# First sublayer's delta rule: one product per doubling step, two per chain step with the state turned, filter products in the last half of the chain

## The reference

```
A = where(strict_low, -einsum('bhnid,bhnjd->bhnij', kb, k), 0)
T = solve_triangular(eye - A, eye, lower=True, unit_diagonal=True)
u = T @ v
w = T @ kb
def step(S, inp):
    attn = where(low, q @ k.T, 0)
    u_i = u - w @ S
    o_i = q @ S + attn @ u_i
    S = S + k.T @ u_i
fir_s = dwconv_causal(v, fir_short_filt)   # 5 taps
fir_l = dwconv_causal(v, fir_long_filt)    # 64 taps
```

## Time and profile before

| what | value |
|---|---|
| median of 3 runs | 3429.51 us (3428.8 to 3432.13) |
| the profiled execution's own time | 3426.57 us |
| its span in the profile | 3424.8 us |
| the stage, from its first matmul to its last copy | 112.7 to 354.5 us |
| granted TensorE clock, mean of the span | 0.878 of full speed |
| PE busy, share of the span | 81% |
| DVE / ACT busy, share of the span | 53% / 40% |

### The profile page before, as it was taken

How to read it: one execution, slowest core, us unless ns; L and a number is a source line. 1 busy time by engine, 2 the same in 40 slices (tenths; PEclk the granted TensorE clock), 3 DMA queues, 4 the chain that set the end, 5 groups by cost and what they waited for, 6 DMA issues and landing times. The chain is left out here.

```text
span 3424.8 us, 57880 instructions
## 1 busy us (share of the span) xinstructions
PE 2778.6 (81%) x22862; PEld 1420.1 (41%) x22862; DVE 1825.0 (53%) x3512; ACT 1380.9 (40%) x2682; POOL 765.7 (22%) x721
## 2 busy tenths in 40 slices
PE   6665778778888768889858889899888988777986
PEld 3454336623336633334332222243233443654546
DVE  4311135369885368830178887611396454537733
ACT  3310434353224337662347777633303233234552
POOL 1000004426535420000245440000361000240003
PEclk8766778978888979999979999999799998887987
DMA  2023001212101231000040220000160001022102
GB/s 114 15 58 85 1 0 43 55 45 74 62 19 46 84 74 33 23 2 0 0 74 15 32 32 1 1 0 12 40 157 13 1 1 50 14 59 69 35 9 74
DMA packets 84405, 130.25 MB, mean 38 GB/s; under 512 B 15584, under 2 KB 52928, under 8 KB 82856
## 3 DMA queue, kind: packets, MB, share of 16 engines
q1 hardware_dynamic: 71528, 106.68, 11.4%
q0 software_dynamic: 9152, 16.71, 2.0%
q10 hardware_dynamic: 3456, 3.15, 0.3%
HBM read 99.93 MB, written 25.85 MB: 37 GB/s over the span
## 5 line engine op out<-in xcount | busy, mean ns | idle before, releaser
L1787 DVE TENSOR_REDUCE at_mp<-PS 128x1 f32<-128x384 f32 (+3 forms) x640 | 306.7, 536 | 85.0 <-PE PS L1610 72.6
L1736 ACT ACTIVATE at_pt<-PS 128x384 f32<-128x384 f32 (+3 forms) x704 | 270.3, 455 | 190.2 <-PE PS L1610 156.5
L1602 PE MATMUL PS<-at_kx,at_qx 48*128 48x384 bf16 (+5 forms) x640 | 198.6, 347 | 60.6 <-DVE at_mp L1787 21.6
L1630 PE MATMUL PS<-at_qx,at_kx 57*128 57x512 bf16 (+5 forms) x704 | 192.8, 314 | 9.7 <-ACT at_pt L1736 9.4
L4235 ACT ACTIVATE ls_pt<-PS,ls_far 128x512 f32<-128x512 f32 x256 | 155.5, 685 | 24.8 <-PE PS L4056 17.9
L4382 DVE CUSTOM_DVE_ANT_0 PS<-PS,ls_pt 128x1024 f32<-128x1024 f32 x128 | 153.9, 1239 | 19.4 <-ACT ls_pt L4235 16.5
L1610 PE MATMUL PS<-at_above,identb 64*128 64x128 bf16 (+1 forms) x1408 | 160.7, 212 | 0.0
L1610 PE MATMUL PS<-at_other,at_eye 64*128 64x128 bf16 (+1 forms) x1408 | 158.2, 208 | 0.0
L2507 DVE TENSOR_TENSOR_SCAN mb_ring<-PS,mb_ring 128x1024 f32<-128x1024 f32 x64 | 146.6, 2291 | 19.3 <-POOL mb_ring L2446 6.7
L2462 PE MATMUL PS<-mb_ring,ident 128*128 128x512 f32 x256 | 149.1, 736 | 5.9 <-DVE mb_ring L2512 5.9
L1113 DVE SCALAR_TENSOR_TENSOR X<-PS,small_L,X 128x512 f32<-128x512 f32 x8 | 6.0, 751 | 261.2 <-PE PS L1061 261.2
(11 more groups left out here) (833 smaller groups left out, 6527.2 us busy)
## 6 DMA issues: line engine op xcount, KB each, us to landing
rw_arena<-rw_v_rows SPq DMA_DIRECT2D x32, 512.0 KB, 4.6
dl_arena<-in_fir_bank SPq DMA_DIRECT2D x32, 256.0 KB, 3.1
lnA<-mb_rows SPq DMA_DIRECT2D x16, 512.0 KB, 3.6
XN<-mb_rows SPq DMA_DIRECT2D x16, 512.0 KB, 3.4
ffn_place<-in_ffn_L SPq DMA_DIRECT2D x4, 1152.0 KB, 17.1
x_rows<-mx_t SPq DMA_DIRECT2D x16, 256.0 KB, 2.4
mx_s<-y_rows SPq DMA_DIRECT2D x16, 256.0 KB, 4.7
ffn_place<-in_ffn_L SPq DMA_DIRECT2D x4, 1024.0 KB, 9.2
```

The source lines that it names most:

```text
L1602: mm = nc.tensor.matmul(PS[:, n % 3, 0:e - c], QX[rows, u % 3, g, blk(i, P)], KX[rows, u % 3, g, c:e], start=True, stop=True)
L1630: mm = nc.tensor.matmul(PS[:, 3 + n % 3, 0:e - c], KX[rows, u % 3, g, blk(j, P)], QX[rows, u % 3, g, c:e], start=True, stop=True)
L1736: nc.scalar.activation(PT[:, y % SLOTS, g, 0:e - c], PS[:, 3 + n % 3, 0:e - c], ACT.Exp, scale=SCALE).then_inc(exp_done, 1)
L1787: nc.vector.tensor_reduce(best, sc, AX.X, ALU.max).then_inc(s_maxed, 1)
```

## The change

`build` makes one product for each step. The square of A is no longer made on PE: ACT copies the square of A' out of the double, and DVE turns it with a 32x32 transpose (`fix`, s = 1 to 4), which gives A squared. Steps 2, 3 and 4 are now one double each. M and G take the places of kb and q side by side (`KBQ`), the outputs go to another buffer (`OD`).

In the chain, PSUM holds the state turned and the output beside it, 64 columns: `corrections(n)` makes u against k and the attention matrix in one set of 8 matmuls, `chain(n)` adds S against M and G in another 8. DVE turns the first half into S (`carry`, a transpose where a copy was) and copies the outputs of each chunk. `corrections(n+1)` is issued right behind `chain(n)`.

The sixteen filter products are taken out of the second half and put behind the links 16 to 31 (`LATER = 16`), on two PSUM banks in turn instead of one. The text of SP's program is not changed, but what it waits for comes later.

```
@@ -2957,10 +2957,10 @@
-        M, U = KBC, VC
+        OD, U = KBC, VC
-        G, OD, S = Q, KB, KK
+        M, G, S = KB, Q, KK
...
@@ -3176,10 +3176,11 @@
-        PRODUCTS = (1, 1, 2, 2, 2, 1, 1, 1)
-        ON_DVE = (4, 1, 2, 2, 1, 1, 0, 2)
+        ON_DVE = (4, 1, 2, 2, 2, 1, 0, 2)
         ON_ACT = (0, 1, 1, 1, 1, 0, 2, 0)
+        ONE_EACH = (1,) * STEPS
+        LATER = 16
...
+            firs_at = lambda n: (n - LATER,) if 0 <= n - LATER < 2 * STEPS else ()
+
+            def carried(n):
+                return PS[:, 4 + n % 2, 0:4 * CH].rearrange("p (b a i) -> p b a i", b=2, a=2)
...
@@ -3260,11 +3252,10 @@
+                    elif s == 1:
+                        single(lo, pw[:, 0, :], pt[:, 0, 0, :])
                     elif s <= 4:
-                        single(hi, pt[:, n % 2, 0, :], pw[:, n % 2, :])
-                        if s in (2, 3):
-                            double(lo, pw[:, n % 2, :], pt[:, n % 2, :, :])
-                        elif s == 4:
-                            single(lo, pw[:, n % 2, :], pt[:, n % 2, 1, :])
+                        double(lo, pw[:, old, :], pt[:, old, :, :])
...
-                def chain(n):
+                def corrections(n):
                     if n % CHUNKS == 0:
                         pe.wait_ge(fixed, upto(ON_DVE, 2 + n // CHUNKS, STEPS - 1))
+                        pe.wait_ge(copied, upto(ON_ACT, 2 + n // CHUNKS, STEPS - 1))
+                    if n >= 2:
+                        pe.wait_ge(o_taken, n - 1)
                     for b in range(2):
                         for h in rows:
+                            mm = nc.tensor.matmul(carried(n)[h, b, :, :], U[h, chunk(b, n)], KA[h, :, chunk(b, n)], start=(b == 0), stop=(n == 0), skip_group_check=True)
+                    return mm
+
+                def chain(n):
+                    pe.wait_ge(s_done, n)
+                    for b in range(2):
+                        for h in rows:
+                            mm = nc.tensor.matmul(carried(n)[h, b, :, :], S[h, chunk(b, n)], KBQ[h, :, chunk(b, n)], start=False, stop=True, skip_group_check=True)
                     mm.then_inc(ks_ready, 1)
+                    if n + 1 < NSTATE:
+                        corrections(n + 1)
...
                 def fir(i):
                     if i == 0:
                         pe.wait_ge(window_done, STEPS)
-                    else:
-                        pe.wait_ge(fir_done, i)
+                    if i >= 2:
+                        pe.wait_ge(fir_done, i - 1)
...
                 for s in range(STEPS):
-                    build(1, s)
-                    chain(2 * s)
-                    fir(2 * s)
-                    build(3, s)
-                    chain(2 * s + 1)
-                    fir(2 * s + 1)
-                for n in range(CHUNKS, NSTATE - 1):
+                    for half, u in enumerate((1, 3)):
+                        n = 2 * s + half
+                        build(u, s)
+                        if n:
+                            chain(n)
+                        else:
+                            first()
+                        for i in firs_at(n):
+                            fir(i)
+                for n in range(CHUNKS, NSTATE):
                     chain(n)
+                    for i in firs_at(n):
+                        fir(i)
...
@@ -3383,62 +3376,50 @@
+                    elif s <= 4:
+                        dve.wait_ge(copied, upto(ON_ACT, u, s))
+                        nc.vector.transpose(pw[:, s % 2, :], pt[:, s % 2, 0, :]).then_inc(fixed, 1)
                         nc.vector.tensor_tensor(c3(pt[:, s % 2, 1, :]), c3(pt[:, 1 - s % 2, 1, :]), half(1), ALU.add).then_inc(fixed, 1)
...
                 def carry(n):
                     dve.wait_ge(ks_ready, n + 1)
+                    if n + 1 < NSTATE:
+                        s = S.rearrange("p (b t) -> p b t", b=2)[:, :, blk(n + 1, CH)]
+                        nc.vector.transpose(s, carried(n)[:, :, 0, :]).then_inc(s_done, 1)
+                    nc.vector.tensor_copy(OD.rearrange("p (b t) -> p b t", b=2)[:, :, blk(n, CH)], carried(n)[:, :, 1, :]).then_inc(o_taken, 1)
```

More of the change, by code:

```diff
@@ L3311, in chain, with first @@
                     mm.then_inc(ks_ready, 1)
-                    if n > CHUNKS:
-                        outputs(n - 1)
+                    if n + 1 < NSTATE:
+                        corrections(n + 1)
+                def first():
+                    corrections(0).then_inc(ks_ready, 1)
+                    corrections(1)
                 def fir(i):
@@ L3322, in fir @@
                         for c in range(PIECE):
-                            mm = nc.tensor.matmul(PS[rows[c], 6, blk(g % 2, P)], XW[:, :, c * 32 + g], RING[:, g % SLOTS, c, :], start=True, stop=True)
+                            mm = nc.tensor.matmul(PS[rows[c], 6 + i % 2, blk(g % 2, P)], XW[:, :, c * 32 + g], RING[:, g % SLOTS, c, :], start=True, stop=True)
                     mm.then_inc(fir_ready, 1)
@@ L3345, in copy @@
                 def copy(u, s):
[L3346 to L3351, removed]
+                    lo = 2 * (u // 2)
+                    pw, pt = POW[:, u // 2], PT[:, u // 2]
+                    if s in (0, 5, 7):
+                        return
+                    act.wait_ge(made, upto(ONE_EACH, u, s))
+                    if s == 1:
+                        nc.scalar.activation(pt[:, 1, 0, :], PS[:, lo, :], ACT.Identity).then_inc(copied, 1)
+                        return
+                    halves = wide(lo).rearrange("p (c a i) -> p c a i", a=2, i=CH)
                     if s == 6:
-                        act.wait_ge(made, first)
                         for a, out in enumerate((pw[:, 1, :], U[:, blk(u)])):
-                            nc.scalar.activation(out.rearrange("p (c i) -> p c i", i=CH), wide(lo).rearrange("p (c a i) -> p c a i", a=2, i=CH)[:, :, a, :], ACT.Identity, scale=0.5).then_inc(copied, 1)
+                            nc.scalar.activation(out.rearrange("p (c i) -> p c i", i=CH), halves[:, :, a, :], ACT.Identity, scale=0.5).then_inc(copied, 1)
+                    else:
+                        nc.scalar.activation(pt[:, s % 2, 0, :].rearrange("p (c i) -> p c i", i=CH), halves[:, :, 0, :], ACT.Identity).then_inc(copied, 1)
                 def window(s):
@@ L3371, in _ @@
                 for s in range(STEPS):
-                    copy(1, s)
-                    take(2 * s)
-                    copy(3, s)
-                    take(2 * s + 1)
+                    for half, u in enumerate((1, 3)):
+                        copy(u, s)
+                        for i in firs_at(2 * s + half):
+                            take(i)
+                for n in range(CHUNKS, NSTATE):
+                    for i in firs_at(n):
+                        take(i)
             @block.vector
@@ L3431, in _ @@
                 for s in range(STEPS):
-                    fix(1, s)
-                    carry(2 * s)
-                    fix(3, s)
-                    carry(2 * s + 1)
-                for n in range(CHUNKS, NSTATE - 1):
+                    for half, u in enumerate((1, 3)):
+                        fix(u, s)
+                        carry(2 * s + half)
+                for n in range(CHUNKS, NSTATE):
                     carry(n)
-                dve.wait_ge(ks_ready, NSTATE)
-                outs(NSTATE // GROUP - 1)
-        POWERS = ARENA[:, 0:8192].rearrange("p (a b c d) -> p a b c d", a=2, b=2, c=4)
+        POWERS = ARENA[:, 2048:10240].rearrange("p (a b c d) -> p a b c d", a=2, b=2, c=4)
         SQ, AB = POWERS[:, 0], POWERS[:, 1]
```

76 lines of the change are left out of this document (15 added, 61 removed).

## The result

The changed kernel takes **3384.1 us** (median of 4 runs, 3375.7 to 3385.1) where the kernel before takes 3429.2 in the same comparison. The ratio is 0.9856, with a 95% interval of 0.9833 to 0.9879, so it is faster by 45 us, 1.4%; 3379 was forecast. The profiled execution took 3383.3 us, its span is 3381.2.

The account below looks back on a forecast made before the run. The stage was taken to be bound by delivery of PE's instructions in packets of 256. Its terms, 60.8 + 74.8 + 40.6 + 15.0 = 191.2 us against 241.8, gave -50.6 and 3379 us; 8-in-10 range 3354 to 3410.

Parts of the forecast that it names:

- First half, -22.4: First half of the stage: 2080 matmul records, 16.25 instruction packets, would take 60.8 us instead of 83.2.
- packets x 3.74: First half: its time is its number of 256-instruction packets times 3.74 us, the price each had before.
- The round trip hidden: First half: a block's way through ACT and DVE, some 2.3 us, hides beside the other block's product, 3.7 us.
- Second half, -49.1: Second half of the stage: 2560 records, 20 packets at 3.74 us, would take 74.8 us instead of 123.9.
- Last stretch: Links 16 to 31 with the moved filter products: 2.8 us for two, 37.8 for 14, together 40.6 us.
- T: Period of the last stretch's other 14 filter products, waiting for filter bank slices: 2.3 to 3.1 us, taken as 2.7.
- Tail, 15.0: Stage's end: storing the last filter product and loading results back, formerly beside the last stretch, now stands bare, 15.0 us.
- The stages behind: Stages after the changed one: same instructions, put at no change, with at most 2 us left for a lower clock.
- Rival 1: Last stretch: slices keep up, packets bind at 1.4 us a link, 22.4 us, 18 less; 3361 us; chance 10%.
- Rival 2: Whole stage: packets are not the bound, pauses are round trips through ACT and DVE; slower, 3440 us; chance 4%.
- Rival 3: Last stretch: instruction packets starve while slices load, costing 49 us; 3428 us, no change or a little slower; chance 8%.
- The three allowances: Spreads above the forecast: 6 us for T, 7 for packet price, 16 for packets and slices holding each other up.

Follow-up runs that it names:

- six slots: The changed kernel with six slots for the filter bank instead of four, so three slice pairs are under way; stage 184.0 us, ratio 0.9837 to the kernel before.

## Why the prediction was right

- *First half, -22.4.* 61.3 us against 60.8. The step "packets x 3.74" held, and was then tested from the other side: eight packets more cost 31 us. The measured price is 3.77.
- *The round trip hidden.* 2.0 us with 2.1 to spare; 1.5 us more on it cost at most 3.9 us. DVE did get a little busier, 17.3 us instead of 16.2, against what was said.
- *Second half, -49.1.* 73.5 us against 74.8. That a packet costs less without slices beside it was right: 3.78 in the run that only moved the filter products, 3.94 in the run that put them back (86.7 / 22), where 3.74 and 3.93 were taken. Here it was 3.68 (73.5 / 20). No run has the turned state without the single products, so what the chain's turn brought by itself is known only from the count of its packets.
- *Last stretch.* T was taken from the middle between a loop of 2.3 us and a throughput of 3.1, and came out at 2.69. The bounds were both wrong in size and the middle was lucky. The loop is longer: from the start of a product to SP's issue it is 1.30 us (254.97 to 256.27) and not 0.74, and a slice lands 4.1 us after its issue under this load, not 3.1. Where the product starts on the first slice of its pair, that gives (1.30 + 4.1) / 2 = 2.7 us. And the DMA engines give more than 214 GB/s: 228 here, and 273 with six slots at 2.24 us.
- *Tail, 15.0.* 14.8 us, read directly from the trace of before.
- *The stages behind at nothing.* 8.0 us in the two profiles, 6 in the medians. At most 2 us were left for a lower clock; PE's busy time at the lower granted clock accounts for the 8.0, and why the clock was lower is not settled. This term is the largest miss, and about the whole difference between 3379 and 3384.
- *The rivals.* Rival 1 (slices keep up) fell: the period is 2.69 us and not 1.4. What was said for it, that the DMA engines are half idle while slices arrive, is not in its rows: the earlier trace rows has them at 0.98 in the microsecond of a load. Rival 2 (packets are no bound) fell by the runs with more matmuls; PE consumes a packet in 1.9 us and gets the next after 3.6 to 3.9. The Trainium skill (Runtime: NRT & Kernel Launch, Instruction fetch mechanics) says that the crossing to the next block is mostly hidden; here the trace does not agree, with 1.6 and 1.9 us of pause before the bursts at 130.84 and 138.03. Rival 3 (packets starve beside slices) did not come: PE's waits in the last stretch in front of the filter products are put down to loads of the bank, and the stretch is as long as these make it.
- *The range.* The three allowances above the forecast, 6, 7 and 16 us, add up to 3408 and not to the 3402 that is written there. Nothing hangs on it here.

## What to carry to other kernels

Where an engine runs many short instructions, count them against the packets of the instruction queue: if bursts of exactly one packet alternate with pauses that no semaphore explains, count instructions and not columns. In this stage a wider matmul then cost what a narrow one did, and a transpose moved to DVE was free because its round trip, 2.0 us, was shorter than the packets beside it. And before a load is moved behind other work, ask what has to wait for its end: here the move alone made the kernel slower, and the other two parts paid for it.

## What the runs showed of the hardware that was not expected

The sixteen DMA engines moved 273 GB/s on the mean of 34 us with three pairs of 256 KB slices under way, at a busy share of 0.87, and 228 GB/s in the last stretch with two. PE's packets were not what the stretch waited for, while beside the 2 MB loaded back in 16 KB pieces PE once paused for 3.37 us in the kernel with the filter products beside the building, and DVE for 8.27 in the kernel before.

PE got its instructions in packets of 256, 16 of them in the first half and 20 in the second, and one came every 3.7 to 3.8 us in the mean of the first half whether the granted clock was 0.71 (83.2 us for 22.25) or 0.86 (61.3 for 16.25).

Identical code behind the stage took 3109.7 to 3133.8 us in four executions on chip B, and 3069.8 and 3077.8 in the two of the first comparison, with PE busy for longer at a lower granted clock in the longer ones, so a stage is better compared by its own length than by the whole.
